# One layer of a message-passing network on one core: equal lanes of edges, a short last pair, and a norm that goes through PSUM

## What is computed

```
h    = relu(layernorm(x))                                  # per node, over 32 features
v    = relu([h[src], h[dst], edge_attr] @ W1 + b1) @ W2 + b2   # per edge, 96 -> 64 -> 32
out  = x + maximum(segment_max(v, dst), h)                 # per node
```

## Time and profile before

| | us |
|---|---|
| median of 3 runs | 3253.02 |
| the profiled execution | 3252.11 |
| its span, first to last instruction | 3250.3 |
| PE busy | 3011.4 |
| DVE busy | 2193.5 |
| ACT busy | 2108.6 |
| POOL busy | 2432.8 |

### The profile page before, as it was taken

One profiled execution on the slowest core, in us unless ns is written; L12 is line 12 of the kernel. 1 busy time (PEld: TensorE's weight loads), 2 busy tenths in 40 slices (PEclk: granted clock), 3 DMA queues, 4 the chain that ended last, 5 costly groups with the idle time before them and its releaser, 6 DMA issues.

```text
span 3250.3 us, 56988 instructions
## 1 busy us (share of the span) xinstructions
PE 3011.4 (93%) x19600; PEld 2222.8 (68%) x19600; DVE 2193.5 (67%) x2408; ACT 2108.6 (65%) x2462; POOL 2432.8 (75%) x2558
## 2 busy tenths in 40 slices
PE   6999999999999999999999999999998998999800
PEld 4777677777777777777777777777676776777500
DVE  6221677777777777777777777777676767777623
ACT  2335677777777777777777777776775776777500
POOL 7777777777777777777777777777777777777746
PEclk9999999999999999999999999999999999999955
DMA  9940333333333333333333333333333333333211
GB/s 303 362 128 27 85 100 99 101 102 99 100 98 99 95 99 100 97 98 97 99 101 100 101 97 99 98 97 84 103 99 80 97 76 109 99 98 97 68 47 26
DMA packets 199047, 338.71 MB, mean 104 GB/s; under 512 B 78486, under 2 KB 122520, under 8 KB 198391
## 3 DMA queue, kind: packets, MB, share of 16 engines
q1 hardware_dynamic: 114866, 293.24, 27.3%
q0 software_dynamic: 81568, 41.91, 10.2%
q10 hardware_dynamic: 2464, 2.14, 0.2%
HBM read 228.49 MB, written 108.59 MB: 104 GB/s over the span
## 4 chain that ended last, share of the span: by engine, by line
PE 87%; DMA 4%; issue 3%; POOL 2%; DVE 2%; SPq 1%; ACT 0%; DVEq 0%; POOLq 0%; ACTq 0%
PE ps_rows L689 66%; PE ps_layers L668 4%; PE ps_layers L670 4%; PE ps_layers L704 3%; PE ps_layers L718 3%; PE ps_layers L727 3%; PE ps_layers L708 3%; PE ps_layers L713 2%; POOL gathered_max L560 2%; DMA picks<-picks_dram 2%; DMA gathered_max<-run_max,gather_ix 1%; POOL src_in L491 1%; DVE onehot L927 1%; DMA src_in<-h_dram,src_ix 0%; DMA dst_i<-in_dst_dram 0%
## 5 line engine op out<-in xcount | busy, mean ns | idle before, releaser
L491 POOL DMA_INDIRECT src_in<-h_dram,src_ix x2304 | 2176.7, 945 | 702.1 <-issue 638.4
L689 PE MATMUL ps_rows<-onehot,table 128*128 128x512 f32 x9800 | 2289.5, 393 | 21.7 <-DVE onehot L927 21.6
L689 PEld LDWEIGHTS ps_rows<-onehot,table 128*128 128x128 f32 x9800 | 1831.0, 188 | 495.9 <-issue 107.2
L620 ACT ACTIVATE onehot<-distance 128x1024 fp32r<-128x1024 bf16 x882 | 878.3, 1049 | 700.6 <-PE ps_rows L689 700.6
L615 ACT ACTIVATE distance<-picks,below_column 128x1024 bf16<-128x1024 int16 x882 | 954.8, 1136 | 52.2 <-DMA picks<-picks_dram 52.2
L927 DVE SCALAR_TENSOR_TENSOR onehot<-picks,column,ps_layers 128x1024 fp32r<-128x1024 int16 x392 | 493.1, 1279 | 365.2 <-PE ps_rows L689 339.0
L668 PE MATMUL ps_layers<-ea_t,rows_in 125*128 125x320 bf16 x980 | 269.1, 302 | 26.4 <-DVE rows_in L793 26.4
L969 DVE STREAM_TRANSPOSE ps_layers<-rows_in 128x512 f32<-128x512 f32 x196 | 129.4, 706 | 231.8 <-ACT hid L606 193.9
L670 PE MATMUL ps_layers<-dst_t,rows_in 125*128 125x320 bf16 x980 | 269.0, 301 | 0.0
L606 ACT ACTIVATE hid<-ps_layers,b_col 128x512 f32<-128x512 f32 x392 | 234.5, 675 | 40.2 <-PE ps_layers L718 40.2
L984 DVE TENSOR_TENSOR_SCAN max_t<-mask_in,max_t,ps_layers 128x512 f32<-128x512 bf16 x196 | 250.5, 1278 | 10.7 <-PE ps_layers L727 7.1
(11 more groups left out here) (108 smaller groups left out, 1107.1 us busy)
## 6 DMA issues: line engine op xcount, KB each, us to landing
picks<-picks_dram SPq DMA_DIRECT2D x98, 512.0 KB
run_max<-rows_in SPq DMA_DIRECT2D x98, 512.0 KB
first_rows<-hid SPq DMA_DIRECT2D x100, 500.0 KB
rows_in<-in_edge_attr_dram SPq DMA_DIRECT2D x98, 384.0 KB
rows_in<-first_rows SPq DMA_DIRECT2D x98, 384.0 KB
src_in<-h_dram,src_ix POOLq DMA_INDIRECT x2304
mask_in<-mask_dram SPq DMA_DIRECT2D x98, 192.0 KB
rows_in<-in_edge_attr_dram SPq DMA_DIRECT2D x98, 128.0 KB
```

The lines of the kernel that those rows point to most:

```text
L491: pool.indirect_dma_start(out=src_in[:, slot, g, r, :], out_offset=None, in_=rows[:, :], in_offset=bass.IndirectOffsetOnAxis(ap=src_ix[:, ...
L620: nc.scalar.activation(onehot[:, RING_AT[c] + BY_DVE[c] + k, :, :].rearrange("p g w -> p (g w)"), distance[:, k, :], ACT.Relu, bias=1.0, s ...
L689: mm = nc.tensor.matmul(ps_rows[g][side][:, 0:WIDE], table[:, i * SIDES + side, part, :], onehot[:, RING_AT[c] + t, g, :], start=(i + part ...
```

## The change

- The lanes become equal: LANE = E / 4 = 100000 edges each, one after the other in DRAM. 97 pairs are full, the last has LAST = 672 edges of each lane: 21 pieces of 32 rows, a full block of 512 and a rest of 160. Its second block has 1 gather in place of 12 (32 columns), and the 4 picks.
- Loads of edges, first rows and mask are one DMA over all lanes in place of two. In the last pair edges and first rows are one DMA per lane, of 21 partitions.
- The store of pair 96 is one DMA per lane, and so is the last store, of 21 partitions.
- The reload of x is issued in `feed` of pair 96, ahead of the stores of pairs 96 and 97.
- The rows that are carried from lane to lane are at the lanes' ends; `place_last` loses seven small instructions.
- The norm's mean and reciprocal are written to PSUM and read from there; the square is an ACT activation between the third and fourth step of the search.
- The picks (`pick_i`) are loaded behind the weights in ACT's queue, with three small DMAs for the last two pairs.
- POOL's gates on `tiles_used` open three tiles sooner (SLACK = 3).
- SP's list of the last two double turns is written out.

```
+LANE = E // A
+STARTS = [a * LANE for a in range(A)]
+LAST = LANE - (PAIRS - 1) * 2 * BLK
+LAST_PARTS = LAST // (2 * R)
+LAST_GATHERED = LAST - BLK - PICKED
+SLACK = 3
...
-            def load_edges(j, slot):
-                for v, lanes in enumerate(lanes_of):
-                    sp.dma_start(ea_rows[chunks(*lanes), slot:slot + 1], ea_view[v][:, :, bass.ds(j, 1)]).then_inc(ea_loaded[slot], D)
+            def load_edges(j, slot, last=False):
+                if last:
+                    for a in range(A):
+                        sp.dma_start(ea_rows[chunk_of_last(a), slot], last_rows(edge_attr, STARTS[a])).then_inc(ea_loaded[slot], D)
+                else:
+                    sp.dma_start(ea_rows[:, slot:slot + 1], ea_view[:, :, bass.ds(j, 1)]).then_inc(ea_loaded[slot], D)
...
+            def store(j, slot, last=False, by_lane=False):
                 sp.wait_ge(max_turned, j * 2 + 2)
                 sp.sem_inc(loads_begun, 1)
-                sp.dma_start(max_view[:, :, bass.ds(j, 1)], max_rows[:, slot:slot + 1]).then_inc(max_stored[slot], D)
+                if last:
+                    for a in range(A):
+                        sp.dma_start(last_rows(run_max, STARTS[a]), max_rows[chunk_of_last(a), slot]).then_inc(max_stored[slot], D)
+                elif by_lane:
+                    for a in range(A):
+                        sp.dma_start(max_view[a][:, bass.ds(j, 1)], max_rows[chunk(a), slot:slot + 1]).then_inc(max_stored[slot], D)
+                else:
+                    sp.dma_start(max_view[:, :, bass.ds(j, 1)], max_rows[:, slot:slot + 1]).then_inc(max_stored[slot], D)
...
+                if end:
+                    load_x()
+                store(j, slot, last, end)
...
-                for b in range(BURSTS):
+                for b in range(BURSTS // 2 + 1 if last else BURSTS):
                     pool.wait_ge(tiles_used, tiles_before + b)
                     pool.sem_inc(gathers_begun, 1)
-                    gather_burst(half, slot, b)
+                    if last and b == BURSTS // 2:
+                        gather_row(half, slot, 1, 0)
+                    else:
+                        gather_burst(half, slot, b)
...
-                    gather_pair(half, slot, turn * (AHEAD * TILES) + (slot + 2 - AHEAD) * TILES)
+                    gather_pair(half, slot, turn * (AHEAD * TILES) + (slot + 2 - AHEAD) * TILES - SLACK, last and slot == AHEAD - 1)
...
+                if j == SQUARE_AT:
+                    act.wait_ge(table_padded, 1)
+                    act.wait_ge(ln_step, 3)
+                    nc.scalar.activation(squared, centred, ACT.Square).then_inc(ln_step, 1)
...
-            V.tensor_scalar(mean[:, :], mean[:, :], 1.0 / F, None, ALU.mult).then_inc(ln_step, 1)
+            V.tensor_scalar(ps_mean, mean[:, :], 1.0 / F, None, ALU.mult).then_inc(ln_step, 1)
...
-            V.tensor_tensor(centred, x_sb[:, :, :], mean[:, :].unsqueeze(2).broadcast_to([P, NJ, F]), ALU.subtract).then_inc(ln_step, 1)
-            dve.wait_ge(ln_step, 3)
-            dve.wait_ge(table_padded, 1)
-            V.tensor_tensor(squared, centred, centred, ALU.mult).then_inc(ln_step, 1)
+            V.tensor_tensor(centred, x_sb[:, :, :], ps_mean.unsqueeze(2).broadcast_to([P, NJ, F]), ALU.subtract).then_inc(ln_step, 1)
...
-            V.reciprocal(rstd[:, :], std[:, :]).then_inc(ln_step, 1)
+            V.reciprocal(ps_rstd, std[:, :]).then_inc(ln_step, 1)
             dve.wait_ge(ln_step, 8)
             V.scalar_tensor_tensor(out=h_sb[:, :, :], in0=centred, scalar=0.0,
-                                   in1=rstd[:, :].unsqueeze(2).broadcast_to([P, NJ, F]),
+                                   in1=ps_rstd.unsqueeze(2).broadcast_to([P, NJ, F]),
                                    op0=ALU.max, op1=ALU.mult).then_inc(h_made, 1)
```

More of the change, by code:

```diff
@@ L29 @@
 TURNS = PAIRS // AHEAD
[L30 to L38, removed]
+LANE = E // A
+assert LANES == F == 32 and E == A * LANE and PAIRS % (2 * AHEAD) == 0 and PAIRS // (2 * AHEAD) > 2
+STARTS = [a * LANE for a in range(A)]
+LAST = LANE - (PAIRS - 1) * 2 * BLK
+LAST_PARTS = LAST // (2 * R)
 PICKS = 4
@@ L44 @@
 PICKED = PICKS * LANES
+LAST_GATHERED = LAST - BLK - PICKED
+assert LAST_PARTS * 2 * R == LAST and LAST_GATHERED == LANES
 WIDE = A * PICKED
@@ L234, in build @@
         ps_rows = [[bank(f"ps_rows{g}{h}") for h in range(SIDES)] for g in range(2)]
+        ps_mean, ps_rstd = (ps_rows[0][n][:, 0:NJ] for n in range(2))
         ps_first = ps_layers[:, 2:4, :]
@@ L424, in _, with load_x, feed @@
             load_picks(2, 0)
[L426 removed]
+            def store(j, slot, last=False, by_lane=False):
                 sp.wait_ge(max_turned, j * 2 + 2)
                 sp.sem_inc(loads_begun, 1)
[L429 to L431 removed]
+                if last:
+                    for a in range(A):
+                        sp.dma_start(last_rows(run_max, STARTS[a]), max_rows[chunk_of_last(a), slot]).then_inc(max_stored[slot], D)
+                elif by_lane:
+                    for a in range(A):
+                        sp.dma_start(max_view[a][:, bass.ds(j, 1)], max_rows[chunk(a), slot:slot + 1]).then_inc(max_stored[slot], D)
+                else:
+                    sp.dma_start(max_view[:, :, bass.ds(j, 1)], max_rows[:, slot:slot + 1]).then_inc(max_stored[slot], D)
+            def load_x():
+                sp.wait_ge(tiles_used, PAIRS * TILES)
+                sp.dma_start(x_again[0:PIECE], x_rows[0:PIECE]).then_inc(x_loaded, D)
+                sp.dma_start(x_again[PIECE:P - 1], x_rows[PIECE:P - 1]).then_inc(x_loaded, D)
+                sp.dma_start(x_again[P - 1:P, 0:TAIL], x_tail).then_inc(x_loaded, D)
+                sp.dma_start(x_again[P - 1:P, TAIL:NJ], x_fill).then_inc(x_loaded, D)
+            def feed(j, k, turn, loads=True, picks=True, indices=True, end=False, before_last=False, last=False, last_indices=False):
                 slot = k % 2
@@ L729, in layer_two, with pair @@
                 mm.then_inc(v_summed, 1)
-            def pair(j, slot, ahead=True):
-                layer_one(j, slot, ahead)
+            def pair(j, slot, ahead=True, last=False):
+                layer_one(j, slot, ahead, last)
                 if ahead:
@@ L748, in _ @@
             for slot in range(2):
-                pair(PAIRS - 2 + slot, slot, ahead=False)
+                pair(PAIRS - 2 + slot, slot, ahead=False, last=slot == 1)
         @block_.vector
@@ L1040, in _, with pair @@
             turn_edges(0, 0, 0)
-            def pair(j, k, turn, again, ahead=True, following=True):
+            def pair(j, k, turn, again, ahead=True, following=True, last_next=False):
                 slot = k % 2
```

146 lines of the change are left out of this document (73 added, 73 removed).

## The result

The changed kernel takes 3228.31 us (median of 6 runs, 3226.88 to 3229.45) where the kernel before, run beside it, takes 3252.18 us (6 runs, 3251.27 to 3254.50). The ratio is 0.9925, with an interval of 0.9914 to 0.9936. The forecast was 3226.7 us, between 3221.0 and 3235.5.

What follows compares the result with a forecast made beforehand. POOL's back-to-back gathers, 1.249 us each, were taken as the bound, not PE at 93% busy. Gains 9.5 + 0.7 + 7.2 + 2.7 + 6.2 = 26.3 us off 3252.1 gave 3225.8, median 3226.7 us, range 3221.0 to 3235.5.

Steps and rivals of the forecast that it cites:

- Part 1: Last pair: 13 gathers in place of 24 remove PE's stop (9.5 us); fewer columns in the source product give 0.7.
- for fewer columns: Pair 97's second-half source products: 32 columns in place of 384 shorten 16 matmuls of 1.59 us, gain 0.7 us.
- Part 2: Norm in the head: PSUM operands and ACT's square remove three long POOL gathers; 7.2 us, carried to the end.
- Part 3: One smaller load in place of two: pair 95's gathered rows land in 5.3 us, not 8.0; gain 2.7 us.
- rival B: Pair 95's gather lands as late as before, other transfers sharing its engines; 3229.4 us, chance 0.2.
- the forecast's 3073.1: Sign in the new trace: PE's layer one of pair 97 begins near 3073.1 us.
- Part 4: Last stores by lane, four DMAs of 21 partitions without x beside them: 4.3 us in place of 10.5, gain 6.2.
- rival D: Last store: four stores are no faster than one, the bytes going through one queue; 3232.9 us, chance 0.12.
- C: Head: PSUM operands don't free POOL, or a new wait at 200 or 363 us eats the 7.2; 3233.9, chance 0.13.
- E: Every pair: single-DMA edges, first rows and masks arrive late, so transfers set PE's period; slower, 3305 us, chance 0.04.

Runs made afterwards that it cites:

- the light kernel: Changed kernel with TensorE's look-up cut to 19 of 100 products a pair, short last pair kept; 3226.61 us, ratio 0.9911 to the kernel before.
- the light pair: Two kernels with TensorE's look-up cut to 19 of 100 products, last pair's gathers short in one, whole in the other; 3226.61 and 3236.51 us.
- the light kernel with whole gathers: Changed kernel with the look-up cut to 19 of 100 products and all 24 gathers in the last pair; 3236.51 us, ratio 0.9942.
- the single edit in the kernel before: Kernel before with only its last store issued lane by lane, four transfers of 32 partitions; 4358.43 us on a slow chip, ratio 0.9954.
- the kernel with whole gathers: Changed kernel, full look-up, last pair's gathers whole (24); on the third chip 4342.47 us, ratio 0.9756.

## Why the prediction was right

**What bounds the kernel.** Right, and the light kernel shows it. The argument was the arithmetic of one row (944 ns and 305 ns of gap, 2500 us / 2003) against the page's busy shares.

**Part 1, 10.2 forecast, 11.95 measured.** The stop went, as forecast, and the light pair gives 9.9 us for the whole last pair. The 0.7 us "for fewer columns" was the wrong reason: the 16 source products take 0.81 us in pair 97, half of them with 32 columns, and 0.85 in pair 96, all with 384. What came in its place was larger, and it is the clock. Pair 97 begins at the lower level in both kernels (granted 0.50 from 3075 to 3077 after, 0.52 from 3082 to 3087 before; its first group takes 2.02 us in both). Then the clock rises in both: it is 1.00 in the window from 3079 above, in which PE works, and 1.00 in the earlier trace rows, in which PE stands. When PE went on there, the clock had fallen again, 0.50 from 3096 to 3103. From the source products' start to the end of the last transposes it is now 9.67 us where it was 11.57.

**Part 2, 7.2 forecast, 6.2 measured at the end of the chain.** The three gathers gave 7.24 us, and POOL reached the scatter 7.34 us sooner. Laid one by one beside the instructions of before, POOL's lead is 7.34 us at its first scatter, 6.24 at its 48th instruction from there, and stays between 6.13 and 6.29 for all that follow. So the microsecond was lost among the first half of the scatters, of which six take 1.14 to 1.65 us (three before, 1.12 to 1.14) and the others 0.97; what they meet wasn't tried. That a gain in the head travels 2800 us unshortened is right, and with no wait at a gate. The last gather of pair 97 came 19.97 us sooner: 13.73 for 11 gathers less, 6.24 for this.

**Part 3, 2.7 forecast, 0.8 measured. This is the step that failed.** It said that one load in place of two, and a smaller one, lets pair 95's rows land as pair 97's did, in 5.3 us. The last gather of pair 95 ended at 3023.78 and DVE had it at 3030.95: 7.2 us after 8.0. The size was chosen against my own rival B, and the traces point at another transfer than the loads: the store.

DVE waits for gathered rows 44 times in four traces: 2 times in the kernel before, once in the one after, 20 and 21 times in the two light ones. Sorted by when SP had last issued a store of the running maxima (512 KB, one piece):

| the store was issued | landings | end of the last gather to rows used | issue of the store to rows used |
|---|---|---|---|
| over 13 us before the gather's end | 6 | 1.3 to 1.5 | |
| 0.5 to 0.7 us before it | 4 | 3.0 to 3.4 | |
| 1.0 us before it | 1 | 5.8 | 6.8 |
| 1.4 to 6.6 us before it | 32 | 5.3 to 9.2 | 10.2 to 12.7 |
| by lane, 8.8 us before it | 1 | 1.5 | |

Rows that meet a store under way are used 10.2 us or more after its issue, as if they waited for its end, since a store in one piece needs about that (10.5 us in part 4). Pair 95 is of this kind in both kernels, 10.55 us after the store of pair 94 before (3027.50) and 10.25 after (3020.70). So were the 5.3 us of pair 97 that I took for an undisturbed landing: the store of pair 96 had been issued 10.24 us ahead of it.
```profile
3085.06 0.58 SPq L429 DMA_DIRECT2D run_max<-rows_in  x1
```
In 30 of the 32 SP issued the next edges 0.7 to 1.0 us behind the store, and the two can't be told apart. But at pair 97 before nothing else was on its way, and at pair 96 of the light kernel with whole gathers only x (from 3055.49 on), and the rows came just so, in the latter 10.64 us after the store. Its gather ended at 3055.60:
```profile
3051.83 0.58 SPq L455 DMA_DIRECT2D run_max<-rows_in  x1
3062.47 0.85 DVE L1004 STREAM_TRANSPOSE src_t<-src_in 128x384 f32<-128x384 f32 x1 [7.59 <-DMA src_in<-h_dram,src_ix]
```
In pair 96 of the light kernel the gather ended at 3053.78, only 0.74 us after the store's issue at 3053.04, and the rows were there at 3057.06. And loads that began with the gather's end held nothing: at pairs 88 and 92 of the light kernel the edges were issued 0.01 and 0.16 us after it, and the rows were there in 3.0 and 3.2 us. Why a store that begins so shortly before the gather's end holds nothing either, no run shows. The change left the store of pair 94 in one piece, and it began 6.8 us sooner where the gather ended 6.3 us sooner, so only 0.8 us was won. This is read from many landings of four traces and not from an edit: the one edit made for it held back the loads and not the store, and it fell on a chip where DVE never waits for a gather. The edit that would test it, that store by lane, has no run on a chip of the first kind.

Since pair 97's layer one hangs on pair 95 (layer one of pair 95 begins 7.08 us sooner, at 3034.39 after 3041.47, and that of pair 97 by the same 7.08), part 2's microsecond less and part 3's 1.9 us less are the whole of the 2.8 us by which 3075.91 missed the forecast's 3073.1.

**Part 4, 6.2 forecast, 6.7 measured.** Right, also in its cause; rival D is refuted by the single edit in the kernel before. The Trainium skill, DMA: Bandwidth & Descriptors, "Why a DMA increments its semaphore by 16 and not by 1", puts the number of engines at the largest number up to 16 that divides the slowest dimension of both sides. By it the store in one piece has 4 engines, one of 32 partitions 16, and one of 21 has 7. The shares of 0.30 and 0.86 agree with 4 and with 16, and for the last stores of 21 partitions the share is 0.35 from 3089 to 3092. They need the same 4.5 us as those of 32 partitions, with two thirds of the bytes.

**The rivals.** C is out: long gathers follow the operand, and POOL waited nowhere. E is out: PE's pace is 27.73 us a pair before and after. B came nearly true, with the store as the transfer that shares the engines. The sum held because two terms were too large by 2.8 us together and two too small by 2.3; that it came within 0.7 us is luck in this part.

## What to carry to other kernels

Divide a stretch by the number of an engine's instructions in it before believing the busy shares: an engine at 75% with a fixed gap behind each instruction can be the bound, and half of the work of one at 93% can go without effect. A stop at the end can cost more than its length: behind one of 9 us TensorE went on at its lower clock, and 1.9 us came on top. And look at how many of the engines a transfer uses, for every transfer that something waits for: 512 KB over a dimension of 4 took 11.2 us from the last transposes to POOL's next gather, four transfers of 32 partitions 4.5. The wait can be that of another: here gathered rows came as late as a store that had nothing to do with them.

## What was not expected of the hardware

A third of the time separates chips: 3252 to 3255 us on the one kind, 4369 to 4454 on the other, with gathers of the same 944 to 948 ns. PE is slower there: before the weight loads of layer one stand pauses that the profile can only call "issue". Here are the waits before those of the dst products (L749, L752) and of the edge products (L745, L748), in the kernel with whole gathers on the third chip and then in the kernel after on its own:
```profile
PEld ps_layers L749 <- issue: 276.4, 380, 2.7
PEld ps_layers L745 <- issue: 265.0, 194, 5.0
```
```profile
PEld ps_layers L748 <- issue: 54.8, 96, 5.0
PEld ps_layers L752 <- issue: 51.7, 196, 0.6
```
541 us against 106, so these two groups are 435 us of the 1100 or so; the granted clock is 0.87 in the mean against 0.97. Where the rest goes wasn't added up, and why these chips do so no run shows.
The same edits rank differently there: eleven gathers more cost nothing that can be seen, and transfers by lane are worth 1.6% on one such chip and 0.5% on another.
